# One attention and feed-forward block on one core: normalisations moved from VectorE to GpSimd, intermediates kept in PSUM

## The reference

```python
x = x + tanh(g_xattn[0]) * attn(layernorm(x), ctx)
x = x + tanh(g_ffn[0]) * ffn(layernorm(x))
# attn: Q = q @ Wq + bq (32 heads of 16); K, V = ctx @ Wk + bk, ctx @ Wv + bv (8 heads of 16,
#       each for 4 heads of Q); softmax(Q K^T / 4) V; then @ Wo + bo
# ffn:  w2 @ (silu(w1 @ x) * (w3 @ x)), inner size 1792; weights with a scale per 128 x 128 block
```

## Time and profile before

| | |
|---|---|
| time, median of 3 runs | 452.72 us (450.8 to 452.84) |
| profiled execution, first to last instruction | 451.3 us |
| TensorE busy | 410.0 us (91%) |
| VectorE busy | 312.5 us (69%) |
| ScalarE, GpSimd busy | 218.9, 152.1 us |

### The profile page before, as it was taken

How to read it: one execution, slowest core, us unless ns; L and a number is a source line. 1 busy time by engine, 2 the same in 40 slices (tenths; PEclk the granted TensorE clock), 3 DMA queues, 4 the chain that set the end, 5 groups by cost and what they waited for, 6 DMA issues and landing times. The chain is left out here.

```text
span 451.3 us, 7299 instructions
## 1 busy us (share of the span) xinstructions
PE 410.0 (91%) x2440; PEld 322.9 (72%) x2440; DVE 312.5 (69%) x510; ACT 218.9 (49%) x392; POOL 152.1 (34%) x125
## 2 busy tenths in 40 slices
PE   3697998989898988788599999999999999999997
PEld 3576776767676776566488788888888888888885
DVE  8778689898989999685959953454446544544524
ACT  5258687878777788552223233233314323323311
POOL 4246466666564757570589600000000000000000
PEclk9778899999999999798799999999999999999999
DMA  7800101010107030000193000000011000000002
GB/s 246 311 24 2 49 2 46 0 46 0 46 0 256 0 141 2 1 1 0 50 421 158 1 0 0 0 0 0 0 55 38 2 0 0 0 0 0 0 0 93
DMA packets 7291, 22.48 MB, mean 50 GB/s; under 512 B 715, under 2 KB 843, under 8 KB 7148
## 3 DMA queue, kind: packets, MB, share of 16 engines
q1 hardware_dynamic: 6844, 21.49, 13.0%
q10 hardware_dynamic: 432, 0.79, 0.5%
HBM read 20.18 MB, written 2.10 MB: 49 GB/s over the span
## 5 line engine op out<-in xcount | busy, mean ns | idle before, releaser
L826 PE MATMUL ps<-x2H,w13H 128*128 128x512 f32 x224 | 90.4, 404 | 3.7 <-DVE w13L L653 3.7
L828 PE MATMUL ps<-x2H,w13L 128*128 128x512 f32 x224 | 89.7, 401 | 0.0
L827 PE MATMUL ps<-x2L,w13H 128*128 128x512 f32 x224 | 89.6, 400 | 0.0
L297 POOL TENSOR_TENSOR PL<-E,PH 128x512 f16<-128x512 f32 x64 | 75.6, 1185 | 37.4 <-ACT PH L413 35.9
L771 DVE SCALAR_TENSOR_TENSOR A<-T,ps 128x512 f32<-128x512 f32 x28 | 19.2, 684 | 54.7 <-ACT T L489 54.7
L489 ACT ACTIVATE T<-ps 128x512 f32<-128x512 f32 x28 | 16.8, 599 | 75.8 <-PE ps L828 75.8
L497 ACT ACTIVATE hH<-hf 128x512 fp32r<-128x512 f32 x28 | 17.7, 632 | 73.6 <-DVE hf L779 73.6
L826 PEld LDWEIGHTS ps<-x2H,w13H 128*128 128x128 f32 x224 | 42.7, 191 | 14.4 <-DVE w13L L653 4.4
L828 PEld LDWEIGHTS ps<-x2H,w13L 128*128 128x128 f32 x224 | 42.7, 191 | 10.7
L653 DVE TENSOR_TENSOR w13L<-wres,w13H 128x1024 fp32r<-128x1024 f32 x28 | 44.5, 1589 | 8.3 <-ACT w13H L392 8.3
L827 PEld LDWEIGHTS ps<-x2L,w13H 128*128 128x128 f32 x224 | 42.7, 191 | 10.1
(11 more groups left out here) (113 smaller groups left out, 801.1 us busy)
## 6 DMA issues: line engine op xcount, KB each, us to landing
wres<-in_wff SPq DMA_DIRECT2D x14, 768.0 KB, 8.8
xn<-in_x SPq DMA_DIRECT2D x8, 256.0 KB, 2.8
X<-in_x SPq DMA_DIRECT2D x1, 2048.0 KB, 11.4
ct<-in_ctxt SPq DMA_DIRECT2D x7, 256.0 KB, 2.6
raw<-in_wproj SPq DMA_DIRECT2D x3, 512.0 KB, 5.2
out<-X SPq DMA_DIRECT2D x6, 256.0 KB, 2.0
raw<-in_wproj SPq DMA_DIRECT2D x1, 1024.0 KB, 5.0
out<-X ACTq DMA_DIRECT2D x2, 256.0 KB, 2.1
```

The lines of the kernel that those rows point to most:

```text
L297: pool.tensor_tensor(PL[:, g % NL, :], E[:, g % NE, :], PH[:, g, :], ALU.subtract).then_inc(pL_ok, 1)
L826: pe.matmul(out_ap, aH, bH, start=start, stop=False)
L827: pe.matmul(out_ap, aH, bL, start=False, stop=False)
L828: return pe.matmul(out_ap, aL, bH, start=False, stop=stop)
```

## The change

- `normalise` and `normalise2` go from VectorE to GpSimd, each right behind the rs it needs (GpSimd L279 and L284 of the new kernel).
- `residual` writes X itself; `keep_x2` goes, and x2n is read from X by `normalise2`.
- The row maxima stay in PSUM (`MX`, in columns 0 to 7 of bank 2), the summed values in PVB (`ONP`), the residue of V in W0 (`VW`). What would overwrite them waits longer: `scores` for mL_ok instead of max_ok, `values` for on_ok instead of pv_read, the stacking of K for v3_ok instead of r1_ok.
- V's three parts and the sums over them are interleaved (element by element, not block by block). `v_first`, `v_rest` and `v_last` follow each other at the end of a step; `pv_norm` follows its `pv_reduce`; `max_high` and `max_low` follow their `max_reduce` for h = 1 and 2.
- All nine steps are written out on all engines.

```diff
+        PVO = PVB[:, 0:8 * VC].rearrange("p (h c) -> p h c", c=VC)
+        ONP = PVB[:, 0:8 * DH].rearrange("p (h d) -> p h d", d=DH)
+        MX = ps[:, 2, 0:2 * GJ].rearrange("p (j g) -> p j g", g=2)
+        VW = W0[:, KVD:2 * KVD].rearrange("p (g d) -> p g d", g=KVH)
...
-            for i in (-1, 0):
-                step(i, i + 2, i + 1, i if i > -1 else None, None)
-            with eng.Fori(1, NBATCH - 2) as i:
-                step(i, i + 2, i + 1, i, i - 1)
-            for i in (NBATCH - 2, NBATCH - 1):
-                step(i, None, i + 1 if i < NBATCH - 1 else None, i, i - 1)
+            def batch(n):
+                return n if 0 <= n < NBATCH else None
+
+            for i in range(-1, NBATCH):
+                step(i, batch(i + 2), batch(i + 1), batch(i), batch(i - 1))
...
+            def normalise(a):
+                pool.wait_ge(rs1_ok, a + 1)
+                pool.tensor_scalar(xn[:], xn[:], mv1[:, 0:1], rs1[:, 0:1], ALU.subtract, ALU.mult).then_inc(xn_ok, 1)
+
+            def normalise2(l):
+                pool.wait_ge(rs2_ok, l + 1)
+                need(pool, x2T_ps, l)
+                pool.tensor_scalar(x2n[:], X[:, l, :], mv2[:, 0:1], rs2[:, 0:1], ALU.subtract, ALU.mult).then_inc(x2n_ok, 1)
...
-                dve.tensor_tensor(vres[:], W0[:, KVD:2 * KVD].rearrange("p (g d) -> p g d", g=KVH), Vp[:, a, :, 0:DH],
-                                  ALU.subtract).then_inc(r1_ok, 1)
+                dve.tensor_tensor(VW, VW, Vp[:, a, :, 0:3 * DH:3], ALU.subtract).then_inc(r1_ok, 1)
+                dve.wait_ge(r1_ok, a + 1)
+                dve.tensor_copy(Vp[:, a, :, 1:3 * DH:3], VW).then_inc(v2_ok, 1)
...
+                dve.tensor_tensor(Vp[:, a, :, 2:3 * DH:3], VW, Vp[:, a, :, 1:3 * DH:3], ALU.subtract).then_inc(v3_ok, 1)
...
-                dve.tensor_reduce(on[:, 8 * q:8 * q + 8, :], v[:, :, 0:3 * DH].rearrange("p h (t d) -> p h d t", t=3),
-                                  AX.X, ALU.add).then_inc(pv_read, 1)
+                dve.tensor_reduce(ONP, PVO[:, :, 0:3 * DH].rearrange("p h (d t) -> p h d t", t=3),
+                                  AX.X, ALU.add).then_inc(pv_read, 1)
...
-                dve.tensor_reduce(mx[:, h, :, :], ps[:, 2:4, :].rearrange("p b (j g k) -> p (b j) g k", j=2, g=2),
+                dve.tensor_reduce(MX, ps[:, 2:4, :].rearrange("p b (j g k) -> p (b j) g k", j=2, g=2),
...
-                dve.scalar_tensor_tensor(out=x2n[:], in0=W2, scalar=tg[:, 0:1], in1=X[:, l, :],
+                dve.scalar_tensor_tensor(out=X[:, l, :], in0=W2, scalar=tg[:, 0:1], in1=X[:, l, :],
...
-                    need(pe, pv_read, 2 * (4 * b + g // 2))
+                    need(pe, on_ok, 4 * b + g // 2)
...
-                    need(pe, max_ok, 4 * f + h)
+                    need(pe, mL_ok, 4 * f + h)
...
-                    pe.wait_ge(r1_ok, f + 1)
+                    pe.wait_ge(v3_ok, f + 1)
```

More of the change, by code:

```diff
@@ L315, in step @@
                     pool.tensor_tensor(rs1[:], ve1[:], neghalf[:], ALU.pow).then_inc(rs1_ok, 1)
+                    normalise(a)
                 if b is not None:
@@ L335, in step @@
                     low(7)
-            attention(pool, step)
+            attention(step)
             scale(2)
@@ L482, in step @@
                     k_high(a)
-            attention(act, step)
+            attention(step)
             def tanh(c, s):
@@ L600, in max_high @@
                 need(dve, mT_ps, 4 * (f - 1) + h + 1)
-                dve.tensor_scalar(Mtok[:, h, :, :, 0], mx[:, h, :, :], -1.0, None, ALU.mult).then_inc(mH_ok, 1)
+                dve.tensor_scalar(Mtok[:, h, :, :, 0], MX, -1.0, None, ALU.mult).then_inc(mH_ok, 1)
             def max_low(f, h):
                 dve.wait_ge(mH_ok, 4 * f + h + 1)
-                dve.scalar_tensor_tensor(out=Mtok[:, h, :, :, 1], in0=mx[:, h, :, :], scalar=-1.0,
+                dve.scalar_tensor_tensor(out=Mtok[:, h, :, :, 1], in0=MX, scalar=-1.0,
                                          in1=r32(Mtok[:, h, :, :, 0]), op0=ALU.mult, op1=ALU.subtract).then_inc(mL_ok, 1)
@@ L625, in statistics2 @@
                 dve.wait_ge(x2_ok, l + 1)
-                dve.bn_stats(st2[:], x2n[:]).then_inc(stats2, 1)
+                dve.bn_stats(st2[:], X[:, l, :]).then_inc(stats2, 1)
                 dve.wait_ge(stats2, l + 1)
-            def keep_x2(l):
-                dve.tensor_copy(X[:, l, :], x2n[:]).then_inc(xcopy_ok, 1)
             def variance2(l):
@@ L662, in _ @@
             dve.memset(r32(Qst[ROWS:P, 2:4, :]), 0.0).then_inc(zeros, 1)
-            normalise(0)
             weights_low(1, KV0, Q0)
@@ L685, in step @@
                     stats(a)
+                if b is not None:
+                    max_high(b, 3)
                 if l is not None:
                     attention_low(l)
-                if f is not None:
-                    dve.wait_ge(r1_ok, f + 1)
-                    dve.tensor_copy(Vp[:, f, :, DH:2 * DH], vres[:]).then_inc(v2_ok, 1)
                 if b is not None:
-                    max_high(b, 3)
+                    max_low(b, 3)
                 if a is not None:
@@ L696, in step @@
                     epsilon(a)
-                if b is not None:
-                    max_low(b, 3)
                 if isinstance(i, int) and i == NBATCH - 2:
                     split13(0, 0, 0)
-                if a is not None:
-                    normalise(a)
                 if f is not None:
@@ L706, in step @@
                     pv_reduce(b, 0)
+                    pv_norm(b, 0)
                 if a is not None:
                     x_low(a)
-                if f is not None:
-                    dve.wait_ge(v2_ok, f + 1)
-                    dve.tensor_tensor(Vp[:, f, :, 2 * DH:3 * DH], vres[:], Vp[:, f, :, DH:2 * DH], ALU.subtract).then_inc(v3_ok, 1)
                 if l is not None:
@@ L722, in step @@
                     epsilon2(l)
-                    keep_x2(l)
                 if b is not None:
                     pv_reduce(b, 1)
-                if l is not None:
-                    normalise2(l)
+                    pv_norm(b, 1)
                 if f is not None:
@@ L730, in step @@
                     max_high(f, 1)
-                if b is not None:
-                    pv_norm(b, 0)
+                    max_low(f, 1)
                 if l is not None:
                     x2_low(l)
-                if f is not None:
-                    max_low(f, 1)
                 if b is not None:
-                    pv_norm(b, 1)
                     pv_reduce(b, 2)
+                    pv_norm(b, 2)
                 if f is not None:
                     max_reduce(f, 2)
-                if b is not None:
-                    pv_norm(b, 2)
+                    max_high(f, 2)
+                    max_low(f, 2)
                 if a is not None:
@@ L746, in step @@
                     k_low(a)
-                if f is not None:
-                    max_high(f, 2)
-                if a is not None:
                     v_first(a)
-                if f is not None:
-                    max_low(f, 2)
                 if a is not None:
                     v_rest(a)
-            attention(dve, step)
+                    v_last(a)
+            attention(step)
             def final(h):
@@ L1035, in step @@
                     pe.wait_ge(w13L_ok, 1)
-                    pe.wait_ge(max_ok, 4 * NBATCH)
+                    pe.wait_ge(mL_ok, 4 * NBATCH)
                     g_or_u(0, 0, 0, 0, range(2))
@@ L1084, in step @@
                     add_bias(W0, 2 * KVD, BK).then_inc(kv_ps, 1)
-            attention(pe, step)
+            attention(step)
             def gu(c, s, h):
```

35 lines of the change are left out of this document (14 added, 21 removed).

## The result

The new kernel takes **458.86 us** (median of 4 runs, 456.71 to 459.17) against 452.78 for the kernel before on the same chip: ratio 1.012, 95% interval 1.009 to 1.015. The forecast was 446.6 with a range of 438 to 455: it is slower, not faster. The profiled execution took 458.94 us, its span 457.2 against 451.3, so +5.9 has to be explained.

A forecast was written before the change was run, and what follows sets the result against it. TensorE alone bounds the kernel from 222 us; before that, attention steps of 21.67 us, with VectorE (20.07 busy) tighter than TensorE. Stage terms sum to -6.1 against the median of 452.72, giving 446.6 us, range 438 to 455.

The forecast's parts named there:

- step -1: Stage before step 0, +0.15 us: scores(0,1) waits 1.3 later for max_low(0,0), half won back at the low clock.
- step 0: First attention step, -2.7 us: xn in time for TensorE, and no fall to half clock there.
- step 7: End of the attention, -5.8 us: VectorE's stretching ends, and split13(1) gets in ahead of GpSimd's scale(2).
- into the feed-forward, and behind it: From on's transposes to gu(2), -8.5 us: gu(2) starts 6.75 earlier, and the half clock behind its wait goes, 1.8.
- clock in the steps: Attention steps, +1.7 us: one fall of TensorE's clock counted for the new waits of 0.3 and 1.4 us.
- Rival C: Slower: TensorE loses its clock in every step from 0 to 6 behind scores(f,0)'s new wait; 456.8 us, chance 0.15.
- scores(f,0): Next batch's first scores: max_low(b,3) behind attention_low lets them start 2.3 us after on's transposes, +1.17 a step.
- scores(f,1): Next batch's second scores: TensorE now waits for max_low(f,0), which stands behind the residual; +1.41 us a step.
- GpSimd's normalisation at 1.04 us: xn and x2n on GpSimd: 1.04 us each, upper bound 1.14, costing nothing up to about 2.5.
- rival B: Before the feed-forward: split13(1) comes after scale(2) began, waits 1.9 us longer, clock falls; about 450 us, chance 0.20.
- V's chain and on: Transposes of on: V's four dependent operations precede the product, TensorE starts at 3.31 against 3.94 us, -0.63 a step.
- counts nothing: Attention loop written out: no effect on time, since the part already written out issues its groups at the loop's distances.

The follow-up runs named there:

- Kernel 9: New kernel with six never-read matmuls of 512 columns on TensorE ahead of scores(f,0) in steps 1 to 6; 449.94 us, ratio 0.992.
- kernel 4: New kernel with max_high and max_low directly behind their reduction at (b,3) and at (f,0), maxima still in PSUM; 448.01 us, ratio 0.987.
- kernel 7: The kernel before with the attention loop written out and nothing else changed; 451.38 us, ratio 0.995.
- kernel 1: New kernel with the row maxima in SBUF again, scores waiting for the reduction (max_ok) and not max_low (mL_ok); 454.65 us, ratio 1.001.
- kernel 3: New kernel with max_high and max_low directly behind their reduction at (f,0) only; 455.13 us, ratio 1.005.
- kernel 6: As kernel 4, with the normalisations back on VectorE except the last one of x2n, left on GpSimd; 440.68 us, ratio 0.971.
- kernel 12: As kernel 6, with scores_t(3) and values(b,0) ahead of scores(f,0) and 15 never-read matmuls in the waits up to step -1; 434.28 us, ratio 0.959.

## Why the prediction was wrong

In the order of its sum, forecast and measured change of each stage (starts of the steps in both traces):

| stage | forecast | measured |
|---|---|---|
| prologue | +1.05 | +1.5 |
| step -1 | +0.15 | +1.4 |
| step 0 | -2.7 | -2.15 |
| step 1 | +2.2 | +3.6 |
| steps 2 to 5 | +4.8 | +10.0 |
| step 6 | +1.0 | +3.0 |
| step 7 | -5.8 | -6.1 |
| into the feed-forward, and behind it | -8.5 | -5.4 |
| clock in the steps | +1.7 | in the rows above |
| sum | -6.1 | +5.9 |

**The step that failed is "Clock in the steps: +1.7 ... I count one".** There was one fall in each of steps 1 to 6. Kernel 9 gives their price: 9.0 us for six, 1.5 each; five more than I counted are, at 1.5 to the 1.7 that I had priced, 7.5 to 8.5 of the 12 us between forecast and result. Rival C had the mechanism, its place and nearly its time (456.8); only step 0 kept its clock. That its time came so near is in part luck: it adds 11.9 us of falls where steps 1 to 6 show 9.0, and misses of other terms, at both ends of the attention, fill the gap. I gave it 0.15 because the settled steps before waited 1.3 us in two pieces and kept the clock. But the new step waits 0.24 and 1.80 where 0.3 and 1.4 were forecast, and the earlier trace rows had already shown a fall behind a wait of 1.49.

**The waits were right, their sizes partly off.** From on's transposes to scores(f,0) it takes 2.69 us where 2.3 was worked out: I let aTL start as soon as ScalarE's aTH was done, but VectorE comes to it only behind the reduction (1.22) and the statistics of xn (0.68), since on now comes early. scores(f,1): 1.04 for 1.41. With the clock held (kernel 9) the step is 22.71 us, where 22.9 was forecast. VectorE is busy for 16.5 us of a step where 15.5 was forecast.

**GpSimd's normalisation at 1.04 us, with 1.14 as the upper bound, was wrong: 2.08 and 2.14.** The bound came from tensor_tensor operations, with one arithmetic step; this is one tensor with two steps and two per-partition operands, which no row of before showed on GpSimd. In the settled steps it hid, as the text said it would up to 2.5 us, but only behind the Mtok waits: that cover went in kernel 4. It showed in steps -1 and 0 (waits of 1.30 and 1.40 for xn) and at the end:

```profile
224.96 2.56 POOL L284 TENSOR_SCALAR x2n<-X,mv,rs 128x512 f32<-128x512 f32 x1
...
227.58 0.66 PE L813 MATMUL ps<-ident,x2n 128*128 128x128 f32 x4 [1.28 <-POOL x2n L284]
...
234.05 3.78 DVE L651 TENSOR_TENSOR w13L<-wres,w13H 128x1024 fp32r<-128x1024 f32 x1
```

That is 1.5 of the 3.1 us missing there. The half clock behind gu(2) did go, but the time went again: the last row is a split stretched beside GpSimd's scales, of which two now come only behind x2n. From 228 to 270 us TensorE waits 1.0 us for such splits and 0.9 for hL, VectorE's low part of h; before, it waited 0.7 us for a split behind gu(2) and nothing for hL. That the later scales cause these waits is argued, not shown by a run.

**Right:** the stretching and its end, VectorE's load not being the bound, step 7, split13(1) and (2) at 1.34 and 1.22 us (so rival B fell), V's chain and on (waits of 0.25 and 0.24). **Right by luck:** no fall in step 0. It was to stay away because xn came in time, but TensorE still waited 1.40 us for xn there. **Off:** the written-out loop "counts nothing": it gains 1.9 us (kernel 7). V's three bf16 parts were priced as before (0.28, 0.22 and 0.27 us); written with a stride they take 0.38 each. In the prologue and step -1, 1.7 us more were lost than forecast, of which some 0.5 is TensorE's wait for xn in step -1 (1.30, where it had waited 0.77 for ScalarE).

The Trainium skill (VectorE: DVE Perf Modes, the section on the TRN2 errata) would, by an estimate from its 120 and 58 cycles, have made each small operation on PSUM 0.06 us dearer. L609 reads PSUM and takes 166 ns; in kernel 1 it reads SBUF and takes 0.17 where nothing stretches it. The runs here don't show the difference.

**Not settled:** what makes the clock fall. Kernel 9 shows that work laid into the wait keeps the clock up, so the wait matters, but its length does not decide alone: 1.80 us is followed by a fall in four steps and not in the fifth (kernel 3), 0.74 in one step of kernel 6, and the waits of 0.68, 0.47 and 0.47 ahead of the fall at 195 us stand in kernel 9 too, without a fall. Also open is why the written-out loop shortens the wait for on.

## What to carry to other kernels

When a buffer moves to a place that another engine writes, the release moves from the first reader to the last one: look at what stands in the queue between the two, and put the last reader directly behind the first. Kernel 4 is the change with two such moves, and it turns a loss of 1.2% into a gain of 1.3%. Count a fall of TensorE's clock for every repetition of a wait, not once. And a wait that goes may uncover the next one: a slow operation that costs nothing behind a wait is to be priced again once that wait is mended.

## What the runs showed of the hardware

- GpSimd's tensor_scalar with two per-partition operands on 128x512 fp32: 2.08 us. Its tensor_tensor of the same size: 1.04 to 1.29. The Trainium skill (GPSIMD Engine Reference, "Engine selection") calls one-input operations on GpSimd roughly line-rate; here VectorE takes a mean of 1.14 (x2n) and 1.36 us (xn) for the same work in kernel 6, GpSimd working beside it, and the measurement decides.
- A fall of TensorE's clock to 0.50 lasts 3.4 to 4 us by the windows, or twice that, and made a step 1.5 to 1.6 us longer (kernels 3 and 9), but only 0.8 in kernel 6's step 5 and 0.6 in the new kernel's step 7. Matmuls whose result nobody reads, laid into the wait, kept the clock at 1.00 in steps 1 to 6 (kernel 9) and from 17 to 28 us (kernel 12).
- VectorE's bf16 write with a stride of three elements: 0.38 us for 128 columns; contiguous 0.28.
